# Transposing most of adj by DMA inside SBUF in place of TensorE transposes, in a two-layer graph kernel on one core

## What is computed

```
h  = relu(layernorm(x))
x1 = x + L0(h, adj)      # 4-bit quantised h @ 3-bit quantised weight, relu, quantised to 4 bits = S; then adj @ S, scaled
g  = relu(layernorm(x1))
A  = D^-1/2 ((adj + adj.T)/2 + I) D^-1/2,   D = row sums of (adj + adj.T)/2 + I
out = x1 + adj @ (A @ g)  # L1: Coefficient2 @ A @ g with Coefficient2 = adj
```

## Time and profile before

| | |
|---|---|
| median of 3 runs | 557.7 us (555.09 to 557.93) |
| the profiled execution, its own time | 555.93 us |
| its span, first to last instruction | 553.9 us |
| mean granted TensorE clock | 0.984 |
| TensorE busy | 516.5 us (93%) |
| DVE, ACT, POOL busy | 264.5, 149.4, 90.0 us |
| DMA | 51.64 MB, mean 93 GB/s |

### The profile page before, as it was taken

The page is one execution under the profiler, slowest core; times in us unless marked ns, Lnnn a source line. Parts: engine busy times, 40 slices in busy tenths (PEclk is TensorE's granted clock), DMA queues, the critical chain, the costliest instruction groups (busy, mean ns, idle before and its releaser), DMA issues.

```text
span 553.9 us, 6745 instructions
## 1 busy us (share of the span) xinstructions
PE 516.5 (93%) x2552; PEld 258.0 (47%) x2552; DVE 264.5 (48%) x392; ACT 149.4 (27%) x206; POOL 90.0 (16%) x56
## 2 busy tenths in 40 slices
PE   2867699999999969999997999999999999999997
PEld 2745355555555624444442444444444444444443
DVE  4996225444354496888889877764000000000000
ACT  1687745444553221232334212214000000000000
POOL 0134599855540000000000000000000000000000
PEclk9999979999999889999998999999999999999999
DMA  6900175544442213223233223300801001001001
GB/s 245 363 0 2 48 243 178 172 148 143 153 141 101 64 57 115 76 76 114 79 111 114 77 91 99 114 0 25 298 20 38 19 19 38 19 19 38 19 19 38
DMA packets 19251, 51.64 MB, mean 93 GB/s; under 512 B 2336, under 2 KB 2336, under 8 KB 19232
## 3 DMA queue, kind: packets, MB, share of 16 engines
q1 hardware_dynamic: 18656, 51.39, 27.7%
q10 hardware_dynamic: 576, 0.00, 0.1%
HBM read 42.99 MB, written 8.39 MB: 93 GB/s over the span
## 4 chain that ended last, share of the span: by engine, by line
PE 81%; DVE 11%; ACT 3%; DMA 2%; issue 2%; POOL 1%; SPq 0%; ACTq 0%; DVEq 0%
PE ps_a L909 30%; PE ps_p L798 18%; PE ps_a L872 6%; PE ps_b L872 6%; PE ps_p L872 6%; PE ps_a L785 3%; PE ps_m L872 3%; PE ps_h L872 3%; PE ps_b L785 2%; DVE split L677 2%; PE ps_b L762 2%; DVE a_in L668 2%; ACT split L423 2%; DVE a_in L667 1%; DMA feat<-in_x 1%
## 5 line engine op out<-in xcount | busy, mean ns | idle before, releaser
L798 PE MATMUL ps_p<-small,at 128*128 128x512 f16 x512 | 120.5, 390 | 5.0 <-DVE feat L610 5.0
L909 PE MATMUL ps_a<-small,at 128*128 128x512 f16 x384 | 85.5, 379 | 0.0
L909 PE MATMUL ps_a<-a_in,at 128*128 128x512 f16 x384 | 85.5, 379 | 0.0
L734 DVE SCALAR_TENSOR_TENSOR feat<-ps_a,feat 128x512 f32<-128x512 f32 x16 | 11.1, 691 | 153.8 <-PE ps_a L909 153.8
L798 PEld LDWEIGHTS ps_p<-small,at 128*128 128x128 f16 x512 | 51.4, 101 | 62.8 <-issue 6.5
L423 ACT ACTIVATE split<-a_in 128x1024 f16<-128x1024 f32 x32 | 33.8, 1057 | 131.1 <-PE ps_p L872 63.7
L909 PEld LDWEIGHTS ps_a<-small,at 128*128 (+1 forms) x384 | 37.6, 98 | 45.3
L909 PEld LDWEIGHTS ps_a<-a_in,at 128*128 (+1 forms) x384 | 37.6, 98 | 45.3
L677 DVE TENSOR_TENSOR split<-a_in,split 128x1024 f16<-128x1024 f32 x32 | 39.2, 1224 | 33.6 <-ACT split L423 33.6
L307 POOL TENSOR_TENSOR at<-at,a_in 128x1024 f32<-128x1024 f32 x20 | 46.8, 2353 | 17.8 <-DMA a_in<-in_adj 17.8
L872 PE MATMUL ps_a<-feat,split 128*128 (+1 forms) x180 | 44.8, 386 | 4.9 <-DVE small L681 3.2
(11 more groups left out here) (124 smaller groups left out, 449.0 us busy)
## 6 DMA issues: line engine op xcount, KB each, us to landing
a_in<-in_adj SPq DMA_DIRECT2D x54, 512.0 KB, 3.8
out<-feat SPq DMA_DIRECT2D x32, 256.0 KB, 2.0
split<-in_adj SPq DMA_DIRECT2D x10, 512.0 KB, 4.2
feat<-in_x SPq DMA_DIRECT2D x8, 512.0 KB, 10.4
feat<-out SPq DMA_DIRECT2D x4, 1024.0 KB, 9.6
at<-in_L_gnn_weight SPq DMA_DIRECT2D x2, 512.0 KB, 5.8
scal<-in_L_gnn_act_alpha ACTq DMA_DIRECT2D x2, 0.5 KB, 6.8
scal<-L_gnn_adj_scaling_factor ACTq DMA_DIRECT2D x1, 0.5 KB, 3.8
```

The costliest lines, as they stand in the source:

```text
L734: nc.vector.scalar_tensor_tensor(xr, BANK[t % 2], 1.0 / (SA * SZ), xr, ALU.mult, ALU.add)\
L798: last = nc.tensor.matmul(l0_bank(r), at_block(r, lo, j), small[:, j * D:(j + 1) * D], start=(j == 0 and lo == 0), stop=(j == T - 1 and lo ...
L909: last = nc.tensor.matmul(BANK[n], at_block(t, lo, j), z_part(j, z_lo), start=(j == 0 and lo + z_lo == 0), stop=(j == T - 1 and lo == 1))
```

## The change

Units 0 to 3 are handled as before. For units 4 to 31 the two f16 parts are made in the layout in which the unit arrives: ACT writes the high part from the input slot to a stage and takes the row sum in the same instruction (`hi_rows`), DVE writes the low part to the stage (`lo_rows`). SP then issues two transposing DMAs from SBUF to SBUF, one for each part, [128, 1024] f16 into eight 128 x 128 blocks of `at`. `turn` for these units, and their reads of PSUM, are gone; 28 of 32 units. There are three stages (two in `split`, one in `tmp`), and a stage is free again when both its DMAs have landed. The ring of input slots has four places in place of six, and units 4 to 7 are loaded ahead into row tiles 8 and 9 of `at`, which are filled later. The column sums are taken after row 12, not in the middle of row 13. SP's order is: for u = 4 to 31, load unit u + 4, then move unit u, and from u = 9 at each odd u a store of x1; then the first four units of the sum. Before the first read of `at` across, DVE waits for the DMAs of units 29 to 31.

```diff
-RING = 6
-EARLY = 6
+RING = 4
+EARLY = 4
+AHEAD = 8
+STAGES = 3
...
+            def free_slot(u):
+
+                if u < EARLY:
+                    sp.wait_ge(turned, u + 1)
+                    sp.wait_ge(rs_done, u + 1)
+                else:
+                    sp.wait_ge(hi_ready, u - EARLY + 1)
+                    sp.wait_ge(lo_ready, u - EARLY + 1)
+                sp.wait_ge(acc_done, u + 1)
+
+            def move(u):
+                if u == UNITS - 2:
+                    sp.wait_ge(col_ps, 1)
+                for lo, ready in ((0, hi_ready), (1, lo_ready)):
+                    sp.wait_ge(ready, u - EARLY + 1)
+                    sp.dma_start_transpose(at_half(u // 2, lo, u % 2).rearrange("p (b i) -> p b i", i=P), stage(u, lo))\
+                      .then_inc(at_moved[u % STAGES][lo], 16)
...
+            for u in range(AHEAD):
+                rows(u)
+            for u in range(EARLY, UNITS):
+                if u + RING < UNITS:
+                    rows_again(u + RING)
+                move(u)
+                if u % 2 and u >= 9:
+                    store_x1((u - 9) // 2)
+            for v, u in ((0, 30), (1, 31), (2, 28), (3, 29)):
+                free_slot(u)
                 sums(v)
...
+            def hi_rows(u):
+                wait_arrived(act, u)
+                if u >= EARLY + STAGES:
+                    wait_moved(act, u - STAGES)
+                if u == EARLY + 2:
+                    act.wait_ge(rs_done, EARLY)
+                nc.scalar.activation(stage(u, 0), unit_in(u), ACT.Copy, scale=SA, accum_out=rowsum[:, u:u + 1])\
+                  .then_inc(hi_ready, 1)
...
-            for u in range(EARLY, UNITS):
-                row_sum(u)
-                if u == UNITS - 2:
-                    act.wait_ge(col_ps, 1)
-                hi_turned(u)
+            for u in range(EARLY, EARLY + 2):
+                hi_rows(u)
             for u in range(EARLY):
                 row_sum(u)
+            for u in range(EARLY + 2, UNITS):
+                hi_rows(u)
...
+            def lo_rows(u):
+                dve.wait_ge(hi_ready, u - EARLY + 1)
+                nc.vector.scalar_tensor_tensor(stage(u, 1), unit_in(u), SA, stage(u, 0), ALU.mult, ALU.subtract)\
+                  .then_inc(lo_ready, 1)
...
+            for u in range(EARLY, AHEAD):
+                lo_rows(u)
             for r in range(12):
-                lo_turned(2 * r + EARLY)
+                lo_rows(2 * r + AHEAD)
                 x1_tile(r)
-                lo_turned(2 * r + EARLY + 1)
+                lo_rows(2 * r + AHEAD + 1)
...
+            for u in range(UNITS - STAGES, UNITS):
+                wait_moved(dve, u)
             sum_unit(0)
...
-                    pe.wait_ge(atlo, 2 * r + 2)
+                    if r < EARLY // 2:
+                        pe.wait_ge(atlo, 2 * r + 2)
+                    else:
+                        wait_moved(pe, 2 * r)
+                        wait_moved(pe, 2 * r + 1)
...
-            for r in range(2, 14):
-                turn(2 * r + EARLY - 2)
-                layer0(r, list(range(B)))
-                turn(2 * r + EARLY - 1)
-                if r == 13:
-                    pe.wait_ge(acc_done, UNITS)
...
+            for r in range(1, 13):
+                layer0(r, list(range(T)))
+            pe.wait_ge(acc_done, UNITS)
```

More of the change, by code:

```diff
@@ L54, in gnn_kernel @@
         split = sb("split", 2 * 2 * W, f16)
-        splitf = split[:, :].bitcast(f32)
         tmp = sb("tmp", 2 * D)
-        junk = tmp[:, 0:D].bitcast(f16)
+        tmpp = tmp[:, :].bitcast(f16)
+        junk = split[:, 0:W]
         ident = sb("ident", P, f16)
@@ L103, in turn_bank @@
         def turn_bank(u):
-            return ps_a if u < EARLY or u % 2 == 0 else ps_b
-        def turn_before(u):
-            return u if u <= EARLY else u - 1
+            return ps_a
         hT_ps_bank = [ps_h[:, :].bitcast(f16), ps_m[:, :].bitcast(f16)]
@@ L122, in gnn_kernel @@
         a_arr = [sem(f"a_arr{k}") for k in range(RING)]
+        a_pre = [sem(f"a_pre{k}") for k in range(AHEAD - EARLY)]
         s_arr = [sem(f"s_arr{k}") for k in range(4)]
@@ L151, in gnn_kernel @@
         atlo = sem("atlo")
+        hi_ready = sem("hi_ready")
+        lo_ready = sem("lo_ready")
+        at_moved = [[sem(f"at_moved{k}{lo}") for lo in range(2)] for k in range(STAGES)]
         acc_done = sem("acc_done")
@@ L176, in unit_in, with before, stage @@
         def unit_in(u):
-            k = u % RING
-            return a_in[:, k * W:(k + 1) * W] if k < 4 else splitf[:, (k - 4) * W:(k - 3) * W]
+            if EARLY <= u < AHEAD:
+                return late(9 - (u - EARLY) // 2, u % 2 * 2 * W, W, f32)
+            return a_in[:, (u % RING) * W:(u % RING + 1) * W]
+        def before(u):
+            return u - AHEAD if u < AHEAD + RING else u - RING
+        def stage(u, lo):
+            k = u % STAGES
+            return tmpp[:, lo * W:(lo + 1) * W] if k == 2 else split[:, (2 * k + lo) * W:(2 * k + lo + 1) * W]
         SLOT = (2, 3, 0, 1)
@@ L210, in z_part, with moved, wait_moved, wait_arrived @@
             return zp[:, (2 * (j - B) + lo) * D:(2 * (j - B) + lo + 1) * D]
-        def arrivals(u):
-            return 16 * (u // RING + 1)
+        def moved(u):
+            first = EARLY + (u - EARLY) % STAGES
+            return 16 * ((u - first) // STAGES + 1)
+        def wait_moved(engine, u):
+            for lo in range(2):
+                engine.wait_ge(at_moved[u % STAGES][lo], moved(u))
+        def wait_arrived(engine, u):
+            if EARLY <= u < AHEAD:
+                engine.wait_ge(a_pre[u - EARLY], 16)
+            else:
+                engine.wait_ge(a_arr[u % RING], 16 * (u // RING + 1 if u < EARLY else u // RING))
         @block.sync
@@ L225, in rows @@
                 sp.dma_start(unit_in(u), adj[(u // 2) * P:(u // 2 + 1) * P, (u % 2) * W:(u % 2 + 1) * W])\
-                  .then_inc(a_arr[u % RING], 16)
+                  .then_inc(a_pre[u - EARLY] if EARLY <= u < AHEAD else a_arr[u % RING], 16)
             def rows_again(u):
-                sp.wait_ge(turned, u - RING + 1)
-                sp.wait_ge(rs_done, u - RING + 1)
-                sp.wait_ge(acc_done, u - RING + 1)
+                free_slot(before(u))
                 rows(u)
+            def free_slot(u):
[13 more added lines that the diff above has]
+                      .then_inc(at_moved[u % STAGES][lo], 16)
             def store_x1(t):
@@ L240, in sums @@
                 sp.dma_start(sum_in(v), adj[j * P:(j + 1) * P, h * W:(h + 1) * W]).then_inc(s_arr[v % 4], 16)
[L242 to L245, removed]
-                sums(v)
[L248 to L261, removed]
+            for u in range(AHEAD):
[8 more added lines that the diff above has]
+                free_slot(u)
+                sums(v)
             store_x1(12)
@@ L327, in row_sum @@
             def row_sum(u):
[L328 removed]
+                wait_arrived(act, u)
                 if u:
                     act.wait_ge(rs_done, u)
[L331 removed]
+                nc.scalar.activation(junk, unit_in(u), ACT.Copy, scale=SA, accum_out=rowsum[:, u:u + 1])\
+                  .then_inc(rs_done, 1)
+            def hi_rows(u):
+                wait_arrived(act, u)
+                if u >= EARLY + STAGES:
[4 more added lines that the diff above has]
+                  .then_inc(hi_ready, 1)
             def hi_turned(u):
@@ L777, in turn @@
             def turn(u):
[L779 to L783, removed]
+                wait_arrived(pe, u)
+                if u:
+                    pe.wait_ge(atlo, u)
                 for k in range(B):
@@ L825, in _ @@
             support(5)
-            turn(4)
             layer0(0, [2, 3])
@@ L838, in _ @@
             layer0(0, [14, 15])
[L839 to L842, removed]
-            for r in range(2, 14):
-                turn(2 * r + EARLY - 2)
-                layer0(r, list(range(B)))
-                turn(2 * r + EARLY - 1)
-                if r == 13:
-                    pe.wait_ge(acc_done, UNITS)
[L849 to L853, removed]
+            for r in range(1, 13):
+                layer0(r, list(range(T)))
+            pe.wait_ge(acc_done, UNITS)
+            for k in range(T):
+                last = nc.tensor.matmul(ps_m[:, k:k + 1], acc[:, k * P:(k + 1) * P], mean_of[:, 0:1],
+                                        start=True, stop=True)
+            last.then_inc(col_ps, 1)
+            layer0(13, list(range(T)))
             layer0(14, list(range(T)))
```

20 lines of the change are left out of this document (8 added, 12 removed).

## The result

| | before | after |
|---|---|---|
| median of the runs | 556.5 us (4 runs) | 567.13 us (566.25 to 567.49, 4 runs) |
| ratio, 95% interval | | 1.0189 [1.0152, 1.0225] |
| profiled execution, own time / span | 555.93 / 553.9 us | 567.37 / 565.8 us |
| row 15 of layer 0 starts | 202.07 us | 213.06 us |
| from there to the end of the span | 351.8 us | 352.7 us |

The changed kernel is 1.9% slower, where a gain was forecast. The date that was predicted, the start of row 15, came 11.0 us late in place of 24 us early, and nearly all of the difference of the spans (11.9 us) is in it.

What follows compares the result with a forecast made beforehand. TensorE alone was taken to bound layer 0; 30 us gained by its terms, 24 us with the DMA engines' pace, so 555.9 - 24 = 532 us profiled, 534 us as median; range 523 to 625 us.

Steps and rivals of the forecast that it cites:

- The step that failed: Layer 0, DMA engines: one transposing move of 256 KB costs 0.85 us, near a plain copy's 0.83 us.
- My own formula: Start of row 15: gain = 24 - 56 (X - 0.83) us, X being the pace of one move, capped at 30.
- The break-even of 1.26 us: Layer 0: at 1.26 us a move the gain is zero, 1.5 times the ordinary pace.
- Rival 4: SP's queue or DMA engines, 64 us to row 15: moves make TensorE wait, slower from 1.31 us a move; chance 0.31.
- TensorE's part: Layer 0: 28 turns vanish, row 0 ends near 63.6 us, rows take 6.90 us; TensorE alone gains at most 35 us.
- I cost them at nothing while the rows take 6.9 us: Per row off TensorE: ACT 2.5, DVE about 4.1, POOL 4.7 us, none becoming the bound; low part 1.22 us.
- The end: Column sums to row 15: moves and first sum loads about 8 us, then 9.25 us unchanged, 17 us together.
- SP's issue: SP's issue of one transposing move lies between 0.42 us, as a store's, and 3.4 us, eight times that.
- The limit of 1.1 us: SP's queue: with loads at 0.33 and stores at 0.42 us, it decides the pace from about 1.1 us an issue.
- The forecast's 530 us for X of 0.7: Whole kernel: a move's pace of 0.7 to 1.0 us gives 530 to 541 us; chance 0.32.
- its cap: Whole kernel: gain limited to 30 us, giving 526 us, when TensorE stays the bound at 0.7 us a move or less.

Runs made afterwards that it cites:

- the run with pieces: Changed kernel with each transposing move replaced by a plain copy whose destination is cut into 1024 pieces of 256 bytes, nothing transposed: 556.38 us (before: 557.7).
- short additions: Changed kernel with POOL adding only 128 of 1024 columns of each unit to the column sums: 564.08 us (one run; before the change: 555.3).
- the thin-load run: Changed kernel loading only the first 128 of 1024 columns of each unit from unit 8 on, all transposing moves kept: 547.88 us (before the change: 555.3).
- the run with copies and other orders: Changed kernel with plain copies for the moves, x1_tile and moves issued earlier, first two sum units loaded before the last two moves: 533.96 us (before: 556.4).
- the last one: Half-turned kernel, moves before loads, with column sums back inside row 13 and work on units 30 and 31 done ahead: 537.62 us, ratio 0.9646 against before the change.

## Why the prediction was wrong

**The step that failed** is the sentence "I take 0.85 us, near the lower end, because the nearest row in kind is a DMA of the same bytes over the same 128 partitions". A transposing move costs 1.58 us of the 16 engines by their busy share and 1.41 us by the pace: the same bytes, but not the same packets. My own formula turns the corrected term into the right sign: 24 - 56 x (1.58 - 0.83) = -18 us by the share, 24 - 56 x (1.41 - 0.83) = -8 us by the pace; measured -11. The break-even of 1.26 us was right as a warning. That the run with pieces (1.24 us by the share) ended 1.3 us from the kernel before is in part luck: by its pace, (4.3 - 2.08) / 2 = 1.1 us, the formula gives a gain of some 8 us, and the start and the end took more than it allows.

**Rival 4** is what happened, at its place and by its mechanism (TensorE waiting for the moves in each row, between 64 us and row 15), with a chance of 0.31 and a price in between its 1.31 and 1.9 us. Only the releaser before each row was DVE's x1_tile and not the move itself, one step further along the chain. The measured time lies in the range of 523 to 625 us, but on the other side of no change.

**TensorE's part was right**: the turns did lie on the path, row 1 started at once (63.96 us, 63.6 predicted), and rows without turns took 6.91 us (6.90). With moves at a copy's price and the orders mended the kernel took the 534 us that I gave, but that hit is partly luck, since errors in it cancel. The column sums ended at 166.7 us and not near 157, 9.7 us late; from there row 15 came after 16.6 us and not 21; and from row 15 to the end it took 349.1 us, not 351.8, as row 15 no longer followed a wait. And 534 us was meant for the median of the runs, 532 for a profiled one like this.

**"I cost them at nothing while the rows take 6.9 us"** was the second wrong step. DVE's low part was priced by a row in which POOL was idle (L667, after 192 us). Beside POOL it took up to 3.4 us, and POOL in turn 3.3 for 2.35. So row 2 started at 79.97 us (73.5 predicted), POOL's ninth sum ended late, SP stood still from 82.7 to 87.1 us, and row 4 started at 102.35 us (89.5 predicted). The Trainium skill (SBUF — State Buffer, Who interferes with whom) says that a VectorE operation with two inputs in SBUF contends with a GpSimd operation that reads SBUF, and the traces agree: before the change DVE's low part read one input from PSUM, took 1.22 us, and POOL 2.35. I did not weigh it. In the changed kernel most of this was hidden behind the moves (short additions gained some 3 us). With cheap moves it is not: POOL and DVE were then busy 59.0 and 56.95 of 59 us. What it costs in that run was not measured; from 542.6 to 534 us it was the orders that changed, and the slow low parts stayed.

**The end**: I allowed 17 us from column sums to row 15; it took 21.0. The loads of the sum were waited for, as I had named, and behind them the moves.

**SP's issue** was bounded by 0.42 and 3.4 us; it is 1.23 to 1.34 us where nothing holds it. The limit of 1.1 us from which I had said that the queue decides does not come out of my own rows: at 3.45 us a unit they give (3.45 - 0.33 - 0.21) / 2 = 1.45 us, and with the other issues and gaps as the thin-load run has them it is (6.91 - 1.83) / 4 = 1.27 us, an estimate. So 1.30 us is at that limit, and the thin-load run shows it as the next bound. (The forecast's 530 us for X of 0.7 does not come out either: the formula gives its cap, 526 us.)

The figure that I quoted from the Trainium skill (DMA: Bandwidth & Descriptors, Latency and other measured facts) for a transposing DMA, 261 GB/s, would be 1.0 us. 256 KB in 1.58 us are 166 GB/s beside other traffic (186 in 1.41 us), so no run here agrees. The other one from the Trainium skill, 1.3 us for a block alone (VectorE: DVE Perf Modes, The three transpose paths), does not add up eightfold: eight blocks took 1.58 us of the engines, and 3.2 us from issue to landing at the shortest.

## What to carry to other kernels

Work that leaves the bound engine lands somewhere: count that place's whole budget per period before the move (here 2.08 us of 3.45 were gone on the DMA engines), and ask how much dearer the new operation may be before it becomes the bound; a reserve of 1.5 times was too thin for an operation without a row. When two places can do the same job and each is over its budget with all of it, divide it: half the transposes on TensorE and half on the DMAs gave 1.8% as first written and 3.5% with its orders mended, where all of them on the DMAs cost 1.9%, and 1.6 to 2.2% with other orders. And before pricing an engine's operation by a row, look what the neighbouring engines did at that moment.

## What was not expected of the hardware

- A transposing DMA of 128 x 1024 f16 inside SBUF took 1.58 us of all 16 engines by their busy share (1.41 us by the pace), a plain copy 0.66, a copy in pieces of 256 bytes 1.24. Its issue on SP took 1.23 to 1.34 us, and up to 3.0 us when the engines were full (once 4.18 us); SP's queue then does nothing else. In the run with pieces it was the loads and stores behind the moves that were held, up to 3.2 us.
- A DVE operation with both inputs in SBUF took 1.22 us with POOL idle and up to 3.4 us with POOL adding; POOL's additions went from 2.35 to 3.3 us. Together they filled both engines in the run with copies and other orders (59.0 and 56.95 of 59 us).
- TensorE's granted clock fell with the waits: 0.87 of the full 2.4 GHz from 63 to 101 us and 0.93 from 101 to 178 us in the changed kernel, 1.00 from 101 to 160 us in the last one. The same column sums took 3.8 us before the change (0.90 granted) and 7.0 us right after a wait of 5.0 us (0.50 granted, the level of 1.2 GHz).
